# Cross attention on one core: VectorE computes the second half's probability low parts before the third eviction

## The reference

```
q = einsum('bcn,dc->bnd', x1, Wq) + bq          # D = 64
k = einsum('bcn,dc->bdn', x2, Wk) + bk[:, None]
v = einsum('bcn,dc->bdn', x2, Wv) + bv[:, None]
attn = softmax(einsum('bnd,bdm->bnm', q, k), axis=2)
out = einsum('bcm,bnm->bcn', v, attn) + x1
```

## Time and profile before

| what | value |
|---|---|
| median of 3 runs | 672.88 us (672.21 to 673.02) |
| the profiled execution | 672.19 us |
| its span, first to last instruction | 670.4 us |
| TensorE busy with matmuls | 650.8 us, 97% of the span |
| VectorE busy | 470.1 us, 70% |
| ScalarE busy | 282.5 us, 42% |
| GpSimd busy | 122.2 us, 18% |
| granted TensorE clock | full in every slice of the span |
| one item in the steady loop (162.80 to 244.01) | 81.21 us |

### The profile page before, as it was taken

One profiled execution on the slowest core, in us unless ns is written; L12 is line 12 of the kernel. 1 busy time (PEld: TensorE's weight loads), 2 busy tenths in 40 slices (PEclk: granted clock), 3 DMA queues, 4 the chain that ended last, 5 costly groups with the idle time before them and its releaser, 6 DMA issues.

```text
span 670.4 us, 8349 instructions
## 1 busy us (share of the span) xinstructions
PE 650.8 (97%) x2848; PEld 532.2 (79%) x2848; DVE 470.1 (70%) x510; ACT 282.5 (42%) x367; POOL 122.2 (18%) x51
## 2 busy tenths in 40 slices
PE   5999999999999999999999999999999999999998
PEld 3877788887888878888788887888878887888886
DVE  5889848778487675786676966769658696486641
ACT  5565513536235443364333743237522456135120
POOL 0302300233003330043100540006300053001100
PEclk9999999999999999999999999999999999999999
DMA  8900722874239631596315862267621875226361
GB/s 310 319 14 4 202 89 79 238 229 117 94 104 287 180 117 63 135 309 167 109 60 137 288 172 94 63 166 266 162 94 63 206 258 162 78 78 142 79 178 58
DMA packets 94874, 100.04 MB, mean 149 GB/s; under 512 B 8336, under 2 KB 69776, under 8 KB 94864
## 3 DMA queue, kind: packets, MB, share of 16 engines
q1 hardware_dynamic: 94864, 99.91, 50.0%
HBM read 51.64 MB, written 16.78 MB: 102 GB/s over the span
## 4 chain that ended last, share of the span: by engine, by line
PE 83%; DVE 8%; issue 5%; ACT 3%; DMA 1%; DVEq 0%; SPq 0%
PE acc_ps L726 39%; PE acc_ps L695 26%; PE s_ps L665 9%; PE s_ps L673 4%; PE s_ps L674 4%; DVE xs_lo L447 2%; DVE full L451 1%; DVE pt_lo L447 1%; ACT q_st L299 1%; ACT cross L299 1%; DMA stage<-in_ctx_dram 1%; DVE probs L489 1%; DVE o_sb L515 1%; PE s_ps L786 1%; DVE blocks L498 1%
## 5 line engine op out<-in xcount | busy, mean ns | idle before, releaser
L726 PE MATMUL acc_ps<-pt_hi,vt_hi 128*128 128x512 f32 x512 | 200.0, 391 | 6.9 <-DVE pt_lo L447 6.9
L726 PE MATMUL acc_ps<-pt_lo,vt_hi 128*128 128x512 f32 x512 | 199.4, 389 | 0.0
L726 PE MATMUL acc_ps<-pt_hi,vt_lo 128*128 128x512 f32 x512 | 199.3, 389 | 0.0
L334 ACT ACTIVATE probs<-s_ps,negmax 128x1024 f32<-128x1024 f32 x64 | 71.4, 1116 | 128.5 <-DVE negmax L482 128.5
L726 PEld LDWEIGHTS acc_ps<-pt_hi,vt_hi 128*128 128x128 f32 x512 | 96.1, 188 | 29.8 <-DVE pt_lo L447 9.9
L726 PEld LDWEIGHTS acc_ps<-pt_hi,vt_lo 128*128 128x128 f32 x512 | 96.1, 188 | 20.1
L726 PEld LDWEIGHTS acc_ps<-pt_lo,vt_hi 128*128 128x128 f32 x512 | 96.1, 188 | 19.8
L268 POOL TENSOR_TENSOR pt_lo<-pt_raw,pt_hi 128x1024 fp32r<-128x1024 f32 x14 | 41.0, 2949 | 364.9 <-ACT pt_hi L299 364.9
L695 PE MATMUL acc_ps<-wv_hi,xs_hi 128*128 128x512 f32 x256 | 99.8, 390 | 0.0
L695 PE MATMUL acc_ps<-wv_hi,xs_lo 128*128 128x512 f32 x256 | 99.6, 389 | 0.0
L695 PE MATMUL acc_ps<-wv_lo,xs_hi 128*128 128x512 f32 x256 | 99.6, 389 | 0.0
(11 more groups left out here) (49 smaller groups left out, 611.6 us busy)
## 6 DMA issues: line engine op xcount, KB each, us to landing
pt_raw<-blocks SPq DMA_DIRECT2D x240, 128.0 KB, 2.4
stage<-in_ctx_dram SPq DMA_DIRECT2D x32, 512.0 KB, 8.8
stage<-in_x_dram SPq DMA_DIRECT2D x32, 512.0 KB, 6.1
o_sb<-in_x_dram SPq DMA_DIRECT2D x64, 256.0 KB, 3.2
out_dram<-o_sb SPq DMA_DIRECT2D x64, 256.0 KB, 2.4
pt_raw<-in_L_xattn_Wv_dram SPq DMA_DIRECT2D x4, 256.0 KB, 8.1
pt_raw<-in_L_xattn_Wk_dram SPq DMA_DIRECT2D x1, 128.0 KB, 3.5
pt_raw<-in_L_xattn_Wq_dram SPq DMA_DIRECT2D x1, 128.0 KB, 7.6
```

The lines of the kernel that those rows point to most:

```text
L334: nc.scalar.activation(probs[:, t % 2, :], s_ps[:, t % 2, :, :].rearrange("p a n -> p (a n)"), ACT.Exp, bias=negmax[:, t:t + 1], accum_out ...
L726: mm = nc.tensor.matmul(acc_ps[:, c % BANKS, :], v[:, m, cols], p[:, m, :], start=(m == 0 and v is vt_hi and p is pt_hi), stop=(m == MT - ...
```

## The change

On VectorE, in the loop and in the last item, the four `p_lo(b, 1, j)` now stand directly behind `low_x2(nb, 1)`. `low_x2(nb, 3)` and `out(b, 0, 2)` follow them, in this order, ahead of `out(b, 0, 3)`. No instruction is added or removed, and no wait is changed.

```
                     low_x2(nb, 1)
-                out(b, 0, 2)
+                for j in range(PAIRS):
+                    p_lo(b, 1, j)
                 if not last:
                     low_x2(nb, 3)
-                for j in range(PAIRS):
-                    p_lo(b, 1, j)
+                out(b, 0, 2)
                 out(b, 0, 3)
```

## The result

| | before | changed |
|---|---|---|
| median of 4 runs | 672.70 us (672.21 to 673.02) | 664.28 us (663.83 to 664.41) |
| the profiled execution | 672.19 us, span 670.4 | 664.22 us, span 662.4 |
| ratio | | 0.9874, 95% interval 0.9857 to 0.9891 |

The changed kernel is 1.3% faster, 8.4 us. 663.8 was forecast, and the range of 662.8 to 666.0 holds it.

A forecast was written before the change was run, and what follows sets the result against it. The prediction took TensorE, with matmuls busy 97% of the span, as the bound. 6 × 1.28 + 0.98 = 8.7 us off gave 663.5 or 664.2 us by scale; it took 663.8, range 662.8 to 666.0.

The forecast's parts named there:

- 1.28 us for an item: TensorE, change of halves: wait's cost per steady item, 1.14 us late start plus 0.14 us lost just behind it.
- Steps 1 and 2: VectorE: `p_lo(b, 1, 0)` starts at 240.95, takes 1.21 us, is ready 0.44 us before TensorE's weight load; wait goes entirely.
- Step 3: Half 1, pairs 1 to 3: low parts ready with margins of 0.7, 0.9 and 1.1 us; no new wait.
- Step 4: VectorE: `low_x2(nb, 3)` ends at 246.75, ahead of the last quarter of `k_next`; cover 4 us, cost zero.
- Step 5: VectorE: `out(b, 0, 2)` moves to about 246.7; `out(b, 1, 0)`, with 1.86 us idle before it, is not delayed; cost zero.
- Step 6: SyncE's queue: tile 2's store goes out 5.8 us later, residuals behind it; cost zero, 5 us cover at the tightest.
- The first item: ScalarE's high part is later there, so 0.4 us of TensorE's wait stays; gain 0.98 us.
- The sum: Six steady items at 1.28 us plus 0.98 us in the first: 8.7 us gained; last item nothing.
- The low part just late: Rival, steady items: 0.1 to 0.4 us of the wait stays, giving 665 to 667.5 us; chance 0.11.
- Given back later: Rival: gain lost later in the item at a load or transfer; half would give 668.2 us; chance 0.04.
- Slower by a late `low_x2(nb, 3)`: Rival: it ends too late for `k_next`; ending at 253.3 would give 680 us; chance 0.02.
- No change by GpSimd: Rival: GpSimd's work slows VectorE's low part to 3.3 us, the wait stays, 672 to 675 us; chance 0.03.

The follow-up runs named there:

- run 2: Kernel before with only `low_x2(nb, 3)` moved behind the four low parts, `out(b, 0, 2)` left ahead of them: 664.76 us.
- Runs 1: Kernel before with only `out(b, 0, 2)` moved behind the four low parts, `low_x2(nb, 3)` left ahead of them: 667.72 us.
- run 6: Changed kernel with `low_x2(nb, 3)` moved further back, behind `out(b, 1, 0)`: 664.13 us.
- run 7: Changed kernel with `low_x2(nb, 3)` behind `out(b, 1, 0)` and done three times instead of once: 680.43 us.
- run 10: Changed kernel once more, unaltered: 663.59 us.
- run 5: Changed kernel with GpSimd's context subtraction of tile 2 done twice, so that it still works under VectorE's first low part: 676.00 us.
- run 3: Kernel before, in its old order, with the context subtraction of tile 3 done twice ahead of the low parts: 686.61 us.

## Why the prediction was right

- **The wait and its place.** Right. TensorE's only idle time in the steady loop was the one at the first matmul of half 1, and it is gone. Of the weight loads' waits only that of the first item is left.
- **1.28 us for an item, not the 0.99 of the idle column.** Right: 5.67 us from the last matmul to the key projection, where it was 6.95. Counting starts caught the 0.14 us behind the restart; run 2 shows that cost alone, at 0.14 to 0.18 us.
- **Steps 1 and 2.** VectorE's first low part stands 1.69 us ahead of the last matmul's start, as worked out (239.37 against 241.06), takes 1.2 us and is 0.4 us early. Runs 1 and 2 put that start at two points between (0.56 and 1.02 us ahead), and TensorE's first matmul of half 1 followed within 0.02 us of what was expected.
- **Step 3.** No wait at a later pair.
- **Step 4.** `low_x2(nb, 3)` ends at 245.12 and is needed at 249.2; run 6 used up the cover without a cost, run 7 went past it and paid.
- **Step 5.** The idle time before `out(b, 1, 0)` went from 1.86 to 0.58 us, 1.28 less.
- **Step 6.** Residuals 1 and 2 went out 5.4 and 7.1 us behind the last matmul's start, and no one waited.
- **The first item.** 0.98 us was the sum. The weight load is 0.31 us late instead of 1.37, and from the last matmul of half 0 to the key projection it is 5.93 us where it was 6.95, a gain of 1.02.
- **The sum.** 8.7 us of the rest of the span. The median moved 8.4 us in the first comparison and 9.4 in the repeat (run 10): the start differs between executions (first value matmul at 15.31 us in the one profile of the changed kernel, 14.49 in the other), which the range allowed for. That the first median came within 0.5 us of the forecast is in part luck; the 8.7 us of the rest is not.
- **The rivals.** The low part just late: not in the steady items. Given back later: no, the item is 79.93 us. Slower by a late `low_x2(nb, 3)`: away here, and 680 us in run 7. No change by GpSimd: away here, and shown by run 5 to give 676 us where it is let in (the rival's own price was 672 to 675). The Trainium skill ("GPSIMD Engine Reference", Key points) speaks of contention of the two engines at their shared interfaces; run 5 agrees, with 3.4 against 1.2 us.

## What to carry to other kernels

When an engine that is never idle makes the bound engine wait, look at what stands ahead of the awaited instruction in its queue and ask of each when its own reader needs it: here an eviction and a subtraction with some 14 and 9 us to spare stood ahead of one that was due. (The eviction's bank had 17 us; a residual whose transfer is queued behind its store landed at 245.14 and was read at 259.45.) Measure such a wait from start to start over the whole stretch, since the idle column leaves out the slower restart. And move work in a queue with the other engines' timetable at hand: the same place is free or costs 2.2 us more by whether GpSimd is at work.

## What the runs showed of the hardware

- **A wait can halve TensorE's clock.** After waits of 2.25 us (run 3) it fell to 1.2 GHz in three of seven cases, for about 3.4 us, at 1.6 us each; after waits of 1.87 us (run 7) in one of seven. Behind the waits of 1.41 us (run 5) and of 0.99 us (before) no fall shows in any of seven. At the start, too, the matmuls begin at the lower rate and change to the full one at different times: the first value matmul of one and the same program start came between 14.49 and 15.86 us of the span. Part of that is the second context tile, whose first matmul started 1.54 to 2.37 us after the one before it.
- **The restart.** Behind a late weight load the first matmul takes 0.50 instead of 0.39 us and the next starts are 0.34 and then 0.23 to 0.24 us apart, where 0.227 is usual. In all it is 0.14 us before and up to 0.18 in run 2, where the matmuls themselves were not idle.
- **VectorE and GpSimd take turns.** A two-operand subtraction of VectorE that meets one of GpSimd's ends 1.1 us after it, as though it had run alone from there: 3.3 to 3.4 us for 1.21. Taking turns is the reading of these times, in the earlier trace rows and in run 5; both engines count as busy all the while.
- **The clock column.** The windows show 1.00 for the first matmuls of the span, while these start 0.43 us apart; the starts are the surer sign there.
